# Local transformer: the output product right behind the scores, the residual sum behind the first shift

## The chip, the cores and the metric

The kernel runs on one core of one Trainium2 chip. The metric is the device time of one execution in microseconds. Five engines work from instruction queues of their own: TensorE (PE, matrix products), VectorE (DVE), ScalarE (ACT), GpSimd (POOL) and SyncE (SP, which here issues all the DMAs). They meet only through semaphores.

## The reference, cut to what matters

The whole program is two layers of a model on 2 x 1024 tokens of 128 features: time mixing with a scan, then a local transformer of depth 6, then full attention, then a mixture of experts. The change touches the local transformer alone:

```python
for i in range(DEPTH):                                   # 6
    x = attn_layer(shift_tokens(x), Wqkv[i], q_scale[i], k_scale[i], Wo[i]) + x
    x = ffn_layer(shift_tokens(x), ln_g[i], ln_b[i], W1[i], b1[i], W2[i], b2[i]) + x

def attn_layer(x, Wqkv, qs, ksc, Wo):                    # 16 heads of 64
    q, k, v = heads(x @ Wqkv)
    q, k = l2norm(q) * qs, l2norm(k) * ksc
    q, k = rotary(q), rotary(k)
    out = local_attention(q, k, v)                       # windows of 32, each sees itself and the one before
    return out @ Wo
```

The moved product is `out @ Wo`, and the moved sum is the `+ x` behind it.

## The kernel before, in words

All of it is unrolled. The local transformer works on groups of 128 tokens: 16 groups (SLOTS) in each of 6 layers, 96 in all, with even groups of one batch and odd ones of the other. A chunk is a pair of groups, and the feed-forward part works on chunks. The order of the work is written out by hand: each engine has a loop over steps i (STEPS), and in a step it does its part for several groups that stand at different depths of the pipeline. What keeps engines apart is semaphores that count finished operations.

A step i of TensorE, in this order (the line is that of the product itself): turn 0 and turn 1, transposes of rotated queries of group i (`turn_qk`, L624); qk 0 and qk 1, projections of group i+2 (`project_qk`, 512 columns each, in three products L607 to L609); turn 2 and 3 for the keys; qk 2 and 3; in odd steps the variance for the feed-forward norm (L717); the attention's output of group i-2 transposed (`turn_att`, L692); the scores of group i (L643 mask, L653, 128 small products); the probabilities of group i-1 transposed (`turn_prob`, L664); one half of v for group i+1 (`project_v`, L607 to L609); in even steps the second feed-forward product (`down`, L735); the other half of v; the value products of group i-1 (`weigh_v`, L682, 128 small ones); in even steps the centre product (L712), in odd ones three pairs of `up` products (L726, L727); last, `project_out` of group i-2 (L704, eight products of the program, 16 passes).

Four banks of PSUM, TURN, are shared in turn by turn, qk, att, prob, v, down, up and out. The dictionary `uses` numbers their uses in TensorE's order, and `wait_free` makes use n wait until the reader of use n-4 is done. Scores and values use three banks of their own.

ScalarE empties turn (L1024), qk (L977), att (L1035), prob (L1030) and v (L1009); it squares queries and keys (L985), takes exponents (L1041), and computes the norms from the sums of squares (L999, L1001, L1003, at the end of a step, for group i+2). In odd steps it also applies the gate's Gelu (L1068), which has a table of its own: one load ahead of it, and one behind it (L1070) for the table of Ln and Exp. In some even steps it splits weights of the next layer (L970).

VectorE in a step: `normalise` of group i+1 (L1296, L1303), first half of `shift_scores` of group i (row maximum L1316, difference L1318), `sum_probs` of group i-1 (L1327; in odd steps it stands ahead of the shift), norm of the feed-forward (L1353, odd) or `finish` (L1367, even, which reads the down product), the second half of `shift_scores`, the sum of squares of group i+2 (L1289), `norm_att` of the first half of group i-1 (L1337), the three `hidden` products (L1359, odd), `add_residual` of group i-2 (L1343), `norm_att` of the second half.

GpSimd rotates group i+1 (L514 products, L519 sums) behind `normalise`, and does the low parts of split weights (L479) and tokens. SyncE issues loads of weights and tokens, the copies of v into windows (`load_v`), and f_x, the feed-forward's input (`load_f_x`, which waits until the residual sums of both groups of a chunk are done).

Of the kernel before, what the change touches and what calls it, by code (L numbers as in the profile page):

```python
# [74 lines left out]
def time_mixing_and_local(nc, A, sb, sem, bank, ident, mean_w, eps, x_main, h_in, h_mid, mod, gate_a):  # L75

    ALL = LAYERS * SLOTS
# [5 lines left out]
    with ExitStack() as ctx:  # L83
# [142 lines left out]
        def live(g):  # L226
            return 0 <= g < ALL

        def even(i, back):
            c = (i - back) // 2  # L230
            return c if (i - back) % 2 == 0 and 0 <= c < CHUNKS else None
# [34 lines left out]
        uses = {}  # L266
        for i in STEPS:
            for a in range(2):
                for j in (2 * a, 2 * a + 1):
                    if live(i):  # L270
                        uses["turn", i, j] = len(uses)
                for j in (2 * a, 2 * a + 1):
                    if live(i + 2):
                        uses["qk", i + 2, j] = len(uses)
            if live(i - 2):
                uses["att", i - 2, 0] = len(uses)
                uses["att", i - 2, 1] = len(uses)
            if i - 2 == ALL - 1:
                uses["out", i - 2, 0] = len(uses)
            if live(i - 1):  # L280
                uses["prob", i - 1, 0] = len(uses)
                uses["prob", i - 1, 1] = len(uses)
            if live(i + 1):
                uses["v", i + 1, 0] = len(uses)
            if even(i, 6) is not None:
                uses["down", even(i, 6), 0] = len(uses)
            if live(i + 1):
                uses["v", i + 1, 1] = len(uses)
            if even(i, 5) is not None:
                for j in range(FB):  # L290
                    uses["up", even(i, 5), j] = len(uses)
            if live(i - 2) and i - 2 < ALL - 1:
                uses["out", i - 2, 0] = len(uses)
        order = list(uses)

        def turn_bank(*use):
            return TURN[uses[use] % len(TURN)]
# [34 lines left out]
        def wait_layer(eng, layer):  # L332
            eng.wait_ge(s_layer[layer % 2], 64 * (layer // 2 + 1))

        with nc.Block(no_gpsimd_drain=True) as blk:
# [264 lines left out]
            def _(pe):  # L600
# [95 lines left out]
                def project_out(g):  # L696
                    layer = g // SLOTS
                    if g % SLOTS == 0:
                        wait_layer(pe, layer)
                    wait_free(pe, "out", g, 0)  # L700
                    pe.wait_ge(S.att_out, 2 * (g + 1))
                    o = bank[:, turn_bank("out", g, 0), 0:BLK]
                    for hp in range(PAIRS):
                        mm = pe.matmul(o, w_o[:, layer % 2, hp, :], att_t[:, g % 2, hp, :], start=hp == 0,  # L704
                                       stop=hp == PAIRS - 1)
                    mm.then_inc(S.out, 1)
# [193 lines left out]
                for i in STEPS:  # L900
                    if i == -1:
                        group_mean(3)
                        project_output(2)
                        second_mean(2)
                        group_var(3)
                        second_var(2)
                    if i == 0:
                        project_output(3)
                        second_mean(3)
                    for a in range(2):  # L910
                        for j in (2 * a, 2 * a + 1):
                            if live(i):
                                turn_qk(i, j)
                        for j in (2 * a, 2 * a + 1):
                            if live(i + 2):
                                project_qk(i + 2, j)
                        if i == 0 and a == 0:
                            second_var(3)
                    if even(i, 5) is not None:
                        variance(even(i, 5))  # L920
                    if live(i - 2):
                        turn_att(i - 2, 0)
                        turn_att(i - 2, 1)
                    if i == ALL + 1:
                        project_out(ALL - 1)
                        last_mean(0)
                    if live(i):
                        scores(i)
                    if live(i - 1):
                        turn_prob(i - 1, 0)  # L930
                        turn_prob(i - 1, 1)
                    if live(i + 1):
                        project_v(i + 1, 0)
                    if i == ALL + 2:
                        center(CHUNKS - 1)
                    if even(i, 6) is not None:
                        down(even(i, 6))
                    if i == ALL + 2:
                        last_var(1)
                    if i == ALL + 3:  # L940
                        last_mean(2)
                    if i == ALL + 4:
                        last_mean(3)
                        last_var(3)
                    if i == ALL + 5:
                        last_mean(4)
                        last_var(4)
                    if live(i + 1):
                        project_v(i + 1, 1)
                    if live(i - 1):  # L950
                        weigh_v(i - 1)
                    if even(i, 4) is not None and i != ALL + 2:
                        center(even(i, 4))
                    if even(i, 5) is not None:
                        for j in range(FB):
                            up(even(i, 5), j)
                    if i == ALL + 1:
                        last_var(0)
                        last_mean(1)
                    if i == ALL + 3:  # L960
                        last_var(2)
                    if live(i - 2) and i - 2 < ALL - 1:
                        project_out(i - 2)

            @blk.scalar
            def _(act):
# [317 lines left out]
            def _(dve):  # L1284
# [255 lines left out]
                for i in STEPS:  # L1540
                    if i == -1:
                        add_logs(3)
                    if live(i + 1):
                        normalise(i + 1)
                    if i == -1:
                        second_scale(2)
                        group_norm(3)
                    if i == 0:
                        second_scale(3)
                        modulation(1)  # L1550
                    if live(i - 1) and even(i - 1, 5) is None:
                        sum_probs(i - 1)
                    if live(i):
                        shift_scores(i, 0)
                    if live(i - 1) and even(i - 1, 5) is not None:
                        sum_probs(i - 1)
                    if i == ALL + 1:
                        last_sum(0)
                        last_sum(1)
                    if even(i, 5) is not None:  # L1560
                        norm(even(i, 5))
                    if i == ALL + 1:
                        add_residual(ALL - 1)
                        last_sum(2)
                    if i == ALL + 2:
                        last_scale(0)
                    if i == ALL + 3:
                        last_scale(1)
                    if even(i, 6) is not None:
                        finish(even(i, 6))  # L1570
                    if i == ALL + 2:
                        last_sum(3)
                    if i == ALL + 4:
                        last_sum(4)
                        last_scale(3)
                    if i == ALL + 5:
                        last_scale(4)
                    if live(i):
                        shift_scores(i, 1)
                    if live(i + 2):  # L1580
                        sum_squares(i + 2)
                    if i == -1:
                        add_output(3)
                    if live(i - 1):
                        norm_att(i - 1, 0)
                    if even(i, 5) is not None:
                        for j in range(FB):
                            hidden(even(i, 5), j)
                    if i == ALL + 3:
                        last_scale(2)  # L1590
                    if live(i - 2) and i - 2 < ALL - 1:
                        add_residual(i - 2)
                    if live(i - 1):
                        norm_att(i - 1, 1)
                dve.wait_ge(S.ff_out, CHUNKS)
# [1078 lines left out]
```

## Time and profile before

| | us |
|---|---|
| median of 3 runs | 2623.19 |
| lowest and highest | 2614.48, 2628.58 |
| the profiled execution's own time | 2625.65 |
| its span | 2623.9 |
| busy: TensorE | 2453.0 (93%) |
| busy: VectorE | 2159.1 (82%) |
| busy: ScalarE | 2037.2 (78%) |
| busy: GpSimd | 1518.5 (58%) |

The span is from the first to the last instruction of one profiled execution. The mean granted clock of TensorE over it is 0.984, where 1 is 2.4 GHz. The local transformer takes most of the span, from about 120 to 1650 us; full attention and the experts follow.

### The profile page before, as it was taken

What the parts mean: (1) busy time and instruction counts of PE and PEld (TensorE: products, weight loads), DVE (VectorE), ACT (ScalarE), POOL (GpSimd) and SP (SyncE); (2) the same over time, 40 slices, a digit from 0 to 9 for tenths busy, and PEclk for the clock granted to TensorE, in tenths of its full rate; (3) what the DMA queues carried; (4) which work ended last, traced back from release to release, by engine and by line L of the source; (5) the groups of instructions that cost most, each with busy time, mean ns of one, the idle gap of its engine ahead of it and who ended that gap; (6) DMA issues with size and microseconds to landing.
All of it is one profiled execution on the core that took longest, in us unless ns stands there. A gap on an engine that the chain in (4) does not pass through costs nothing. (4 is left out here: it accounts for less than half of the span.)

```text
span 2623.9 us, 118567 instructions
## 1 busy us (share of the span) xinstructions
PE 2453.0 (93%) x52349; PEld 1966.4 (75%) x52349; DVE 2159.1 (82%) x2455; ACT 2037.2 (78%) x4077; POOL 1518.5 (58%) x1029
## 2 busy tenths in 40 slices
PE   6799999999999999999999999689999999997999
PEld 2488888888888888888888887467676776775787
DVE  5888888888888888888888887388888888885888
ACT  4688888889889888888888887566666666764676
POOL 3788887888788878888788785122222232322111
PEclk9899999999999999999999999899999999999999
DMA  3243433443334334333433333122222222221221
GB/s 96 56 94 92 106 77 92 92 106 83 93 93 113 80 89 102 96 83 93 97 94 79 85 85 71 36 54 52 60 61 58 50 61 60 57 53 34 82 73 41
DMA packets 275793, 202.01 MB, mean 77 GB/s; under 512 B 117568, under 2 KB 215880, under 8 KB 274248
## 3 DMA queue, kind: packets, MB, share of 16 engines
q1 hardware_dynamic: 275280, 194.42, 30.9%
q8 instruction: 414, 6.78, 1.1%
q14 instruction: 99, 0.81, 0.1%
HBM read 36.96 MB, written 1.11 MB: 15 GB/s over the span
## 5 line engine op out<-in xcount | busy, mean ns | idle before, releaser
L514 POOL TENSOR_TENSOR lt_t_sin<-lt_qk,lt_tab 128x512 f32<-128x512 f32 x384 | 682.8, 1799 | 243.9 <-DVE lt_qk L1296 241.8
L519 POOL TENSOR_TENSOR lt_qr<-lt_qr,lt_t_sin 128x1024 f32<-128x1024 f32 x192 | 457.8, 2385 | 28.2 <-POOL lt_t_sin L514 0.5
L2078 DVE TENSOR_REDUCE fa_neg_max<-bank 128x1 f32<-128x1024 f32 x256 | 301.6, 1220 | 94.7 <-PE bank L1875 93.3
L1901 PE MATMUL bank<-fa_prob_t,fa_v 32*64 32x128 f32 x16384 | 295.9, 277 | 18.9 <-issue 14.0
L2000 ACT ACTIVATE fa_prob<-bank,fa_neg_max 128x1024 f32<-128x1024 f32 x128 | 142.7, 1115 | 217.5 <-DVE fa_neg_max L2078 165.2
L1901 PEld LDWEIGHTS bank<-fa_prob_t,fa_v 32*64 32x64 f32 x16384 | 245.8, 131 | 81.3 <-issue 60.5
L2088 DVE STREAM_TRANSPOSE fa_prob_t<-fa_prob 128x1024 f32<-128x1024 f32 x256 | 302.1, 1219 | 0.0
L607 PE MATMUL bank<-lt_w_high,lt_x_high 128*128 128x512 f32 x576 | 262.8, 456 | 0.8 <-ACT lt_v_tok L1009 0.4
L1296 DVE TENSOR_TENSOR lt_qk<-lt_qk,lt_rn 128x2048 f32<-128x2048 f32 x96 | 236.3, 2461 | 5.9 <-ACT lt_rn L1003 2.2
L1289 DVE TENSOR_REDUCE lt_ssq<-lt_qr 128x32 f32<-128x2048 f32 x96 | 218.9, 2281 | 23.0 <-ACT lt_qr L985 23.0
L1303 DVE TENSOR_TENSOR lt_qr<-lt_qk,lt_tab 128x2048 f32<-128x2048 f32 x96 | 232.7, 2424 | 3.3
L977 ACT COPY lt_qk<-bank 128x512 f32<-128x512 f32 x384 | 220.4, 593 | 18.2 <-POOL lt_t_sin L514 2.8
L608 PE MATMUL bank<-lt_w_low,lt_x_high 128*128 128x512 f32 x576 | 228.4, 396 | 0.0
L609 PE MATMUL bank<-lt_w_high,lt_x_low 128*128 128x512 f32 x576 | 227.8, 396 | 0.0
L1316 DVE TENSOR_REDUCE lt_row_max<-bank 128x8 f32<-128x512 f32 x192 | 131.7, 686 | 113.4 <-PE bank L653 113.4
L624 PE MATMUL bank<-ident,lt_qr 128*128 128x128 f32 x1536 | 201.1, 274 | 14.7 <-POOL lt_qr L519 12.6
L985 ACT ACTIVATE lt_qr<-lt_qk 128x1024 f32<-128x1024 f32 x192 | 203.4, 1060 | 0.0
L624 PEld LDWEIGHTS bank<-ident,lt_qr 128*128 128x128 f32 x1536 | 177.5, 141 | 31.4 <-POOL lt_qr L519 15.7
L704 PEld LDWEIGHTS bank<-lt_prob_t,lt_w_o 128*128 128x128 f32 x1536 | 186.7, 192 | 8.1 <-issue 1.5
L704 PE MATMUL bank<-lt_prob_t,lt_w_o 128*128 128x128 f32 x1536 | 187.6, 275 | 1.0 <-ACT lt_prob_t L1035 0.8
L1807 POOL TENSOR_TENSOR fa_att_t<-fa_att,fa_inv_all 128x512 f32<-128x512 f32 x32 | 40.6, 1270 | 245.4 <-ACT fa_att L2024 245.4
L682 PEld LDWEIGHTS bank<-lt_v,lt_prob_t 64*32 64x32 f32 x12288 | 130.1, 105 | 66.7 <-issue 65.1
(260 smaller groups left out, 5912.5 us busy)
## 6 DMA issues: line engine op xcount, KB each, us to landing
lt_v<-lt_v_tok SPq DMA_DIRECT2D x576, 128.0 KB
fa_v<-fa_v_tok SPq DMA_DIRECT2D x256, 128.0 KB, 2.7
lt_v<-lt_v_tok SPq DMA_DIRECT2D x192, 64.0 KB
lt_k_t<-lt_k_t SPq DMA_DIRECT2D x84, 128.0 KB, 2.7
lt_v<-lt_v SPq DMA_DIRECT2D x168, 64.0 KB, 2.1
lt_w_raw<-in_lt_wqkv_dram SPq DMA_DIRECT2D x36, 256.0 KB
ex_cw_all<-cw_kept SPq DMA_DIRECT2D x8, 1024.0 KB, 4.5
lt_x_s<-h_in SPq DMA_DIRECT2D x96, 64.0 KB, 2.7
```

The lines of the kernel that those rows point to most:

```text
L514: pool.tensor_tensor(dst[:, :, i, :], src[:, :, 1 - i, :], tab[:, g // 2 % 2, 1, at:at + 32].unsqueeze(1).to_broadcast([P, HEADS, 32]), AL ...
L519: pool.tensor_tensor(qr[:, g % 2, half], qr[:, g % 2, half], t_sin[:, :], ALU.add).then_inc(S.rotated, 1)
L607: pe.matmul(o, xh, w_high[:, k % WS, :], start=True, stop=False)
L608: pe.matmul(o, xh, w_low[:, k % WS, :], start=False, stop=False)
L609: return pe.matmul(o, xl, w_high[:, k % WS, :], start=False, stop=True)
L624: mm = pe.transpose(bank[:, turn_bank("turn", g, j), n * P:(n + 1) * P], qr[:, g % 2, (4 * j + n) * P:(4 * j + n + 1) * P], ident[:, :])
L704: mm = pe.matmul(o, w_o[:, layer % 2, hp, :], att_t[:, g % 2, hp, :], start=hp == 0, stop=hp == PAIRS - 1)
L1296: dve.tensor_tensor(heads, heads, r.unsqueeze(2).to_broadcast([P, 2 * HEADS, HD]), ALU.mult)\
L1303: dve.tensor_tensor(qr[:, g % 2, :].rearrange("p (a h d) -> p a h d", a=2, h=HEADS), qk[:, g % 2, :].rearrange("p (a h d) -> p a h d", a=2 ...
L1901: mm = pe.matmul(bank[d, 4 + a, 0:P].rearrange("p (u r) -> p u r", u=UPQ), v[rows, half % 2, kb, d], prob_t[rows, q % 2, par, :, 32 * kb:3 ...
L2078: dve.tensor_reduce(neg_max[:, u % 2, par:par + 1], bank[:, 2 * par:2 * par + 2, :].rearrange("p a n -> p (a n)"), AX.X, ALU.max, negate=T ...
L2088: dve.transpose(prob_t[:, q % 2, par, u % UPQ, :], prob[:, u % 2, par, :]).then_inc(S.turned, 1)
```

## The change

The call of `project_out(i - 2)` moves on TensorE from the end of the step to the place right behind `scores(i)`, ahead of `turn_prob(i - 1, 0)`. The call of `add_residual(i - 2)` moves on VectorE from between `hidden` and the second `norm_att` to right behind `shift_scores(i, 0)`. The list `uses` moves its entry of "out" along, to stand behind "att" and ahead of "prob", so that the numbering of bank uses stays that of TensorE's order; with it every use behind "att" in the step gets another bank and another predecessor. The last group (ALL - 1) had its own, earlier place already and keeps it. No instruction is added or taken away.

```diff
@@ uses
             if live(i - 2):
                 uses["att", i - 2, 0] = len(uses)
                 uses["att", i - 2, 1] = len(uses)
-            if i - 2 == ALL - 1:
+            if live(i - 2):
                 uses["out", i - 2, 0] = len(uses)
@@
                 for j in range(FB):
                     uses["up", even(i, 5), j] = len(uses)
-            if live(i - 2) and i - 2 < ALL - 1:
-                uses["out", i - 2, 0] = len(uses)
@@ TensorE
                     if live(i):
                         scores(i)
+                    if live(i - 2) and i - 2 < ALL - 1:
+                        project_out(i - 2)
                     if live(i - 1):
                         turn_prob(i - 1, 0)
@@
-                    if live(i - 2) and i - 2 < ALL - 1:
-                        project_out(i - 2)
@@ VectorE
                     if live(i):
                         shift_scores(i, 0)
+                    if live(i - 2) and i - 2 < ALL - 1:
+                        add_residual(i - 2)
                     if live(i - 1) and even(i - 1, 5) is not None:
                         sum_probs(i - 1)
@@
-                    if live(i - 2) and i - 2 < ALL - 1:
-                        add_residual(i - 2)
                     if live(i - 1):
                         norm_att(i - 1, 1)
```

## Rows read from the trace of the kernel before

**Rows 1.** Busy time by stretch: us of stretch, then each engine; PEclk, DMA share, GB/s.
```profile
900.00:1100.00 200.00, 192.56 (x4177) 164.26 (x4175) 167.47 (x178) 176.62 (x328) 163.08 (x92) 1.00 0.41 96
```

**Rows 2.** Waits of TensorE, 140 to 1660 us: total us, times, longest.
```profile
PE bank L682 <- issue: 24.7, 25, 1.9
PE bank L664 <- ACT lt_prob L1041: 13.7, 23, 1.8
PE bank L653 <- issue: 4.7, 6, 2.5
```

**Rows 3.** Timeline, TensorE, odd into even step: start, us, what; idle before in brackets.
```profile
1023.05 0.59 PE L727 MATMUL bank<-lt_f_norm,lt_w 128*85 128x256 f32 x2
1023.48 1.95 PE L704 MATMUL bank<-lt_prob_t,lt_w_o 128*128 128x128 f32 x16
1025.27 1.04 PE L624 MATMUL bank<-ident,lt_qr 128*128 128x128 f32 x8
...
1027.54 1.03 PE L624 MATMUL bank<-ident,lt_qr 128*128 128x128 f32 x8
1028.33 0.48 PE L607 MATMUL bank<-lt_w_high,lt_x_high 128*128 128x512 f32 x1
```

**Rows 4.** Timeline, ScalarE, the same boundary.
```profile
1023.69 0.47 ACT L1068 ACTIVATE lt_f_gate<-bank,lt_lvec 85x256 f32<-85x256 f32 x1 [0.39 <-PE bank L727]
1024.18 1.28 ACT L1070 ACT_TABLE_LOAD   x1
...
1026.31 0.57 ACT L1024 COPY lt_q_t<-bank 128x512 f32<-128x512 f32 x1
...
1027.26 0.60 ACT L977 COPY lt_qk<-bank 128x512 f32<-128x512 f32 x1
```

**Rows 5.** Timeline, TensorE, the even step and into the next.
```profile
1031.10 1.48 PE L653 MATMUL bank<-lt_k_t,lt_q_t 64*32 64x64 f32 x128
1033.19 1.09 PE L664 MATMUL bank<-ident,lt_prob 128*128 128x128 f32 x8 [0.61 <-ACT lt_prob L1041]
...
1036.91 1.48 PE L682 MATMUL bank<-lt_v,lt_prob_t 64*32 64x64 f32 x128
...
1042.92 1.03 PE L624 MATMUL bank<-ident,lt_qr 128*128 128x128 f32 x8
1043.71 0.48 PE L607 MATMUL bank<-lt_w_high,lt_x_high 128*128 128x512 f32 x1
```

**Rows 6.** Timeline, VectorE, the end of the even step.
```profile
1036.33 0.49 DVE L1367 SCALAR_TENSOR_TENSOR h_in<-bank,lt_lvec,h_mid 128x256 f32<-128x256 f32 x1 [0.77 <-PE bank L735]
...
1038.05 2.27 DVE L1289 TENSOR_REDUCE lt_ssq<-lt_qr 128x32 f32<-128x2048 f32 x1
...
1040.85 0.29 DVE L1343 TENSOR_TENSOR h_mid<-h_in,bank 128x128 f32<-128x128 f32 x1
```

**Rows 7.** Timeline, ScalarE, even into odd step.
```profile
1040.36 0.32 ACT L999 ACTIVATE lt_rn<-lt_ssq,lt_least 128x32 f32<-128x32 f32 x1 [1.40 <-DVE lt_ssq L1289]
...
1041.47 0.58 ACT L1024 COPY lt_q_t<-bank 128x512 f32<-128x512 f32 x1
...
1042.50 0.59 ACT L977 COPY lt_qk<-bank 128x512 f32<-128x512 f32 x1
```

**Rows 8.** Timeline, TensorE, value products of two odd steps.
```profile
1053.80 0.27 PE L682 MATMUL bank<-lt_v,lt_prob_t 64*32 64x64 f32 x2 [1.59 <-issue]
...
1273.40 1.09 PE L664 MATMUL bank<-ident,lt_prob 128*128 128x128 f32 x8
...
1275.83 1.17 PE L682 MATMUL bank<-lt_v,lt_prob_t 64*32 64x64 f32 x96
1278.90 0.46 PE L682 MATMUL bank<-lt_v,lt_prob_t 64*32 64x64 f32 x32 [1.90 <-issue]
```

**Rows 9.** Timeline, GpSimd, end of the second rotation.
```profile
1039.80 2.37 POOL L519 TENSOR_TENSOR lt_qr<-lt_qr,lt_t_sin 128x1024 f32<-128x1024 f32 x1
```

**Rows 10.** Busy time in the stretch behind the hole of 1.90 us.
```profile
1280.40:1283.70 3.30, 3.30 (x10) 2.27 (x9) 0.97 (x2) 0.95 (x2) 2.46 (x2) 0.50 0.26 60
```

## The prediction

> **What bounds the kernel now.** I read the busy time of the engines in a stretch of the local stage first. TensorE is busy 192.56 of 200 us there, ScalarE 177, VectorE 167, GpSimd 163 [rows 1]. So TensorE sets the pace and an edit can give back only its few idle microseconds. The waits of TensorE over the whole stage (140 to 1660 us) say what those are: 24.7 us inside the value products L682 and 4.7 us inside the scores L653, both with nobody to wait for ("issue"), and 13.7 us ahead of the probability transposes L664, on the exponent [rows 2]. The moved product L704 appears in no large wait: where it stands it waits for nothing.
>
> The timeline then shows a strict pattern of two steps. An odd step ends with the three "up" products, an even one with the centre product; both then run L704, and the next step starts. L704 holds TensorE for 1.79 us, from 1023.48 to the next start at 1025.27, and as long in the other step [rows 3]. Meanwhile other engines do what the start of the next step needs. The question is therefore less what the product fills at its new place than what it covered at the old one.
>
> **What is needed at a step's start.** The four turning banks go round: use n waits until use n-4 is emptied. A step begins turn 0, turn 1, qk 0, qk 1, turn 2, turn 3, qk 2, qk 3. So turn 2 waits for ScalarE's copy of turn 0, and qk 2 for its copy of qk 0, and TensorE reaches turn 2 only 2.27 us after its step began (1025.27 to 1027.54). The change alters no link among these eight.
>
> *Odd to even.* The last up product starts at 1023.05; the gate on it at 1023.69, after ScalarE idled 0.39 us for it, so this chain is released by TensorE. Behind it on ScalarE without a hole: gate, 1.28 us of table load at 1024.18, three small norm operations, two copies of turned queries, and the copy of qk 0 from 1027.26 to 1027.86 [rows 4]. TensorE starts qk 2 at 1028.33 [rows 3]. Spare: 0.47 us. With L704 gone from between, TensorE arrives 1.79 us sooner after the up product, while the chain is as long as before. It needs about 0.05 us from a copy's end to the start (the exponent's release shows such a lag). Stall: 1.79 - 0.47 + 0.05 = 1.37 us. Of this 1.2 us show already at turn 2 (the copy of turn 0 ends at 1026.88, turn 2 starts at 1027.54), the rest at qk 2.
>
> *Even to odd.* Here VectorE carries it. The "down" product is followed by the sum L1367 at 1036.33, for which VectorE idled 0.77 us; then the second shift and the sum of squares from 1038.05 to 1040.32 [rows 6]. ScalarE idled 1.40 us for that sum, then runs the norms, the square L1045, two copies (the first from 1041.47 to 1042.05), and the copy of qk 0 from 1042.50 to 1043.09 [rows 7]. TensorE starts qk 2 at 1043.71 [rows 5]: 0.62 us to spare. The down product stands behind the new place of L704 too, so again the anchor comes 1.79 us nearer: 1.79 - 0.62 + 0.05 = 1.22 us.
>
> I read these two spares step by step. In 39 of 44 even steps the first is 0.5 to 0.6 us; in the other five, at the end of a layer, a weight copy on ScalarE leaves 0.05. In 41 of 44 odd steps the second is 0.5 to 0.6 us, in three 0.2. Each odd step from 5 on has the gate behind it and each even one from 6 on the down product, so 45 boundaries of each kind count: 45 x (1.37 + 1.22) = 116.6 us, and the tighter ones add 5 x 0.4 + 3 x 0.4 = 3.2. **Cost: 120 us.** Both anchors are on TensorE and lie behind the preceding stall, so one stall does not pay for the next. Lower bound: if only half came through, 60; upper: no spare at all, 1.79 at each, 161.
>
> **What the new place gives.** In an even step the scores end near 1032.6, and the transposes L664 start at 1033.19 after 0.61 us idle [rows 5]. The exponent that they wait for stands behind split copies and copies of the turned attention. With 1.79 us of product between, the wait is covered: 18 even steps lose about 0.7 us now, the others 0 to 0.4. In the row they are 13.7 us [rows 2]: **-14 us** (bounds 10 and 20).
>
> The product itself waits at its new place for the attention's copies out of the turning banks (ScalarE, which works on them while the scores run) and for bank use n-4, now qk 2: long emptied. Cost nothing; without the cover some tenths a step. Its first weight load waits no more than before.
>
> The "issue" idle is a second gain. It comes in the middle of 128 identical tiny products, as 96 of them, 1.90 us of nothing, then 32 [rows 8]. It falls nearly all in odd steps, where from the transposes L664 to L682 there are 2.43 us (1273.40 to 1275.83) [rows 8]; in even steps the down product makes that 3.72 us (1033.19 to 1036.91) [rows 5], with the wait ahead of it, and the idle is nearly gone. I take it that instructions arrive no faster, and two bursts of 256 instructions stand too close. The move puts 1.79 us (and 32 instructions) between them. Of 29.4 us [rows 2], which may be somewhat more with idle under the table's threshold, I take **-22 us** (bounds 0 and -35).
>
> The Trainium skill, "Runtime: NRT & Kernel Launch", section "Instruction fetch mechanics", speaks against this term: it says that fetch is hidden, since the sequencer issues more slowly than its buffer fills. By it the idle would have another cause, nothing says that it would shrink, and the sum would be 22 us higher. The trace has idle without a releaser in the burst, so I weigh the page as a rival only.
>
> **The other moved parts.** add_residual is 0.29 us of VectorE, at 1040.85 of the even step [rows 6], where it used to hold up the second norm_att. Now it stands behind the first shift and may wait there: shift done some 1.5 us after the scores, product 1.8 us and its signal after them, so up to 0.5 us of waiting. Behind it are queued sum_probs or the layer's norm, finish and the second shift. In even steps finish waits 0.77 us for the down product anyway, and that comes later too: hidden. In odd steps the second shift feeds only the next scores: hidden. Without that cover it is 0.5 us in 96 steps. The freed end of the step does not start normalise sooner, since that also waits for the norms, which come later by the chains above.
>
> GpSimd's rotation follows normalise. Its last sum ends at 1039.80 + 2.37 = 1042.17 and turn 2 of the odd step starts at 1042.92 [rows 5, 9]: 0.75 us spare. The rotation moves 1.8 us later, TensorE 1.37 - 0.68 later in this step: short by 0.4 us, under the 1.0 us that turn 2 then waits for ScalarE anyway. Cost nothing, unless the bank chain is shorter than I think; then 0.4 us in 20 steps.
>
> Bank uses shift: down waits for the residual sum in its own step (done some 2.4 us after the scores; the transposes and a projection still lie ahead of down), and qk 1 of even steps for the last hidden product, just in time, and if late, under the wait that follows at turn 2. SyncE's f_x load waits for the sum that is now earlier, and its value loads, issued behind v's copy, are 1.8 us later with a step to go before use. Nothing for either.
>
> **Sum.** On the profiled execution's own 2625.65 us (span 2623.9): + 120 - 14 - 22 = 2709.6 us. That execution lies 2.5 us above the median of the runs, so 2707; since some stalls will give instruction supply time ahead of the scores, I take 2704 us, 3.1% slower.
>
> **Rivals.**
> - *The boundary absorbs the loss* (faster, 0.07). The single mechanism: ScalarE's and VectorE's chains run earlier than rows 4, 6 and 7 tell, because they are not released by the up and down products. Then only the gains count: 2623 - 14 - 22 = 2587. It decides where the delay of the qk 0 copy is under 0.5 us. Against it: the idle rows directly ahead of the gate, of L1367 and of L999 show all three waiting. A half-way version, with one of the two boundaries free, gives 2707 - 55 = 2652 (0.12).
> - *Supply idle stays* (0.17): 2704 + 22 = 2726. For it: only an inference from spacing backs the gain.
> - *The clock falls* (0.06). In one step the 1.90 us hole in L682 is followed by a stretch of granted clock 0.50, 3.3 us long, and 1.00 again behind it [rows 8, 10]. At half clock such a stretch loses some 1.7 us. If one pair in two brought it: 2704 + 24 x 1.7 = 2745. Against it: the hole of 1.59 us at 1052 lies in 200 us of clock 1.00 [rows 1, 8], with the 0.61 us holes of that stretch; the new ones are under 1.4 us. The Trainium skill, "TensorE: Matmul & The Clock Gate", section "A second HAM failure mode: psum-queue depth-cycling", describes just this, short idle at each turn of the banks that makes the clock swing; the trace has so far not borne it out.
> - *Nothing moves* (0.04): the product is 1.8 us wherever it stands, and all is absorbed: 2620.
>
> **Numbers.** Forecast 0.54 at 2704. The range from 2650 takes in one free boundary, and up to 2735 lost supply gains. Under about 0.5% this kernel's measurement can't tell a change. Faster 0.07, same 0.04, slower 0.89.
>
> **What would show it.** Right: waits of TensorE L624 on ScalarE's copy lt_q_t L1024, some 1 us, in nearly every step, 90 or more in all, with a smaller one at L607; the wait of L664 on the exponent gone; the issue idle in L682 well under 24.7 us; TensorE busy down to 182 to 186 of 200 us in the stretch of rows 1; pairs of steps 1.5 to 2 us longer. Wrong: L624 without such waits, or waiting on GpSimd's lt_qr instead; clock 0.5 in the stage's windows; a wait of L704 itself on lt_prob_t.

## The result and the profile after

The changed kernel takes 2719.78 us (median of 4 runs, 2713.29 to 2722.47) against 2625.89 us (2614.48 to 2633.98) for the kernel before, measured with it. The ratio is 1.0357, 95% interval 1.0313 to 1.0402: 3.6% slower. The profiled execution has a span of 2719.3 us, 95.4 us more than before. Its lines from the bank numbering on stand two lower: L622 is the L624 of before (turn), L702 the L704 (output product), L680 the L682 (value products), L651 the L653 (scores).

The instructions are the same in number and kind. TensorE is busy 91% instead of 93%, in the stretch of [rows 1] 187.45 us instead of 192.56, at the same granted clock:

```profile
PE 2484.1 (91%) x52349; PEld 1960.2 (72%) x52349; DVE 2145.8 (79%) x2455; ACT 2015.7 (74%) x4077; POOL 1517.3 (56%) x1029
```
```profile
900.00:1100.00 200.00, 187.45 (x4004) 156.01 (x4003) 156.59 (x172) 162.64 (x305) 153.01 (x89) 1.00 0.35 82
```

TensorE's waits in the local stage, here 140 to 1760 us, answer to [rows 2]:

```profile
PE bank L622 <- ACT lt_q_t L1022: 79.0, 89, 1.6
PE bank L651 <- issue: 12.5, 15, 2.3
PE bank L680 <- issue: 10.8, 20, 2.1
PE bank L622 <- POOL lt_qr L517: 4.0, 3, 1.5
...
PE bank L702 <- issue: 3.7, 7, 0.7
```

A wait that is not in [rows 2] now comes 89 times: turn 2 waits for ScalarE's copy of turn 0. The wait of 13.7 us on the exponent is gone. The idle without a releaser (called supply idle below) is no longer mainly inside the value products; the scores now have more of it.

The odd-to-even boundary answers to [rows 3, 4]. First TensorE, then ScalarE. The up product is now followed at once by turn 0, and turn 2, due 2.27 us later, comes 3.54 us later (1082.45 to 1085.99), 0.14 us after ScalarE's copy of turn 0 (from 1085.28, 0.57 us, the first of the two in the row) has ended. The third up product still releases the gate, and the chain behind it has kept its length:

```profile
1082.02 0.59 PE L725 MATMUL bank<-lt_f_norm,lt_w 128*85 128x256 f32 x2
1082.45 1.32 PE L622 MATMUL bank<-ident,lt_qr 128*128 128x128 f32 x8
...
1085.99 1.07 PE L622 MATMUL bank<-ident,lt_qr 128*128 128x128 f32 x8 [0.65 <-ACT lt_q_t L1022]
1086.87 0.50 PE L605 MATMUL bank<-lt_w_high,lt_x_high 128*128 128x512 f32 x1
```
```profile
1082.65 0.47 ACT L1066 ACTIVATE lt_f_gate<-bank,lt_lvec 85x256 f32<-85x256 f32 x1 [0.27 <-PE bank L725]
1083.14 1.28 ACT L1068 ACT_TABLE_LOAD   x1
...
1085.28 1.05 ACT L1022 COPY lt_q_t<-bank 128x512 f32<-128x512 f32 x2
...
1086.22 0.60 ACT L975 COPY lt_qk<-bank 128x512 f32<-128x512 f32 x1
```

The copy of qk 0 ends at 1086.82, and the product that needs its bank starts at 1086.87: the spare of 0.47 us is used up. Note the bracket: 0.65 us, while the start is 1.27 us late. The group of turn 0 and 1 has itself become longer (1.32 instead of 1.04 us), as turn 1 waits a little for VectorE's first hidden product, which reads the bank that turn 1 needs; such pieces of a late start stand in no bracket of turn 2. The distance between two starts is the safer reading.

The even-to-odd boundary answers to [rows 5 to 7], TensorE, VectorE, ScalarE:

```profile
1098.56 1.04 PE L622 MATMUL bank<-ident,lt_qr 128*128 128x128 f32 x8
...
1101.90 1.06 PE L622 MATMUL bank<-ident,lt_qr 128*128 128x128 f32 x8 [0.90 <-ACT lt_q_t L1022]
```
```profile
1093.15 0.29 DVE L1341 TENSOR_TENSOR h_mid<-h_in,bank 128x128 f32<-128x128 f32 x1 [0.47 <-PE bank L702]
...
1096.03 0.48 DVE L1365 SCALAR_TENSOR_TENSOR h_in<-bank,lt_lvec,h_mid 128x256 f32<-128x256 f32 x1 [1.17 <-PE bank L733]
...
1097.76 2.27 DVE L1287 TENSOR_REDUCE lt_ssq<-lt_qr 128x32 f32<-128x2048 f32 x1
```
```profile
1100.07 0.32 ACT L997 ACTIVATE lt_rn<-lt_ssq,lt_least 128x32 f32<-128x32 f32 x1 [1.41 <-DVE lt_ssq L1287]
...
1101.18 1.06 ACT L1022 COPY lt_q_t<-bank 128x512 f32<-128x512 f32 x2
```

The copy of turn 0 again is the first of the last row's two (0.58 us), and turn 2 again starts 0.14 us after its end. The residual sum waits 0.47 us at its new place, and that costs nothing here: VectorE then waits 1.17 us for the down product in any case.

For the experiments I call the time from the start of turn 0 to the start of turn 2 the head of a step. It is 2.27 us where nothing waits (0.87 us in step 94, which has no projection between). Summed over 45 even steps (6 to 94) and 44 odd ones (7 to 93):

| kernel | heads even | heads odd | supply idle (L682, L653) |
|---|---|---|---|
| before | 101.1 | 100.0 | 24.7, 4.7 |
| changed | 159.5 | 144.7 | 10.8, 12.5 |

### The profile page after: what moved, and what is told of

It is laid out like the page before. It is cut to its first block and busy times, and to the rows that moved or that the text cites. A ratio compares the mean times of both kernels' runs of the same rounds, so it can differ in the third digit from the quotient of the medians.

```text
span 2719.3 us, 118567 instructions
## 1 busy us (share of the span) xinstructions
PE 2484.1 (91%) x52349; PEld 1960.2 (72%) x52349; DVE 2145.8 (79%) x2455; ACT 2015.7 (74%) x4077; POOL 1517.3 (56%) x1029
## 5 line engine op out<-in xcount | busy, mean ns | idle before, releaser
L1899 PEld LDWEIGHTS bank<-fa_prob_t,fa_v 32*64 32x64 f32 x16384 | 246.8, 131 | 78.7 <-issue 58.4
L622 PE MATMUL bank<-ident,lt_qr 128*128 128x128 f32 x1536 | 210.9, 277 | 96.7 <-ACT lt_q_t L1022 81.1
L622 PEld LDWEIGHTS bank<-ident,lt_qr 128*128 128x128 f32 x1536 | 172.7, 142 | 156.2 <-issue 101.6
L1294 DVE TENSOR_TENSOR lt_qk<-lt_qk,lt_rn 128x2048 f32<-128x2048 f32 x96 | 222.1, 2313 | 48.6 <-ACT lt_rn L1001 48.4
L1028 ACT COPY lt_prob_t<-bank 128x512 f32<-128x512 f32 x192 | 103.3, 590 | 176.5 <-PE bank L662 176.5
L975 ACT COPY lt_qk<-bank 128x512 f32<-128x512 f32 x384 | 214.1, 629 | 6.3 <-POOL lt_t_sin L512 2.8
L1314 DVE TENSOR_REDUCE lt_row_max<-bank 128x8 f32<-128x512 f32 x192 | 131.6, 686 | 101.1 <-PE bank L651 100.9
L702 PE MATMUL bank<-lt_prob_t,lt_w_o 128*128 128x128 f32 x1536 | 199.4, 283 | 5.3 <-issue 3.7
L702 PEld LDWEIGHTS bank<-lt_prob_t,lt_w_o 128*128 128x128 f32 x1536 | 180.6, 193 | 15.7 <-issue 7.3
```

The lines of the kernel that those rows point to most:

```text
L622: mm = pe.transpose(bank[:, turn_bank("turn", g, j), n * P:(n + 1) * P], qr[:, g % 2, (4 * j + n) * P:(4 * j + n + 1) * P], ident[:, :])
L1294: dve.tensor_tensor(heads, heads, r.unsqueeze(2).to_broadcast([P, 2 * HEADS, HD]), ALU.mult)\
L1899: mm = pe.matmul(bank[d, 4 + a, 0:P].rearrange("p (u r) -> p u r", u=UPQ), v[rows, half % 2, kb, d], prob_t[rows, q % 2, par, :, 32 * kb:3 ...
```

## The experiments

Ratios are to the kernel before, timed on the same chip beside each experiment, with the 95% interval in brackets; a time in us is the median. The medians of before were 2622 to 2633, so across experiments the ratio is the safer measure. Diffs are shortened, with ... for what is left out. The waits shown are those of 140 to 1680 us.

**e1, the new places in even steps only.** Both calls and the entry of "out" get a condition:

```diff
-                    if live(i - 2) and i - 2 < ALL - 1:
+                    if live(i - 2) and i - 2 < ALL - 1 and i % 2 == 0:
                         project_out(i - 2)      # behind scores(i); with != at the step's end
```

> The kernel before, with the product and the residual sum at their new places in even steps only; odd steps end with the product as before. Theory (cover at the step boundary): only the even-to-odd boundary loses its cover. In the changed kernel the heads of odd steps (start of turn 0 to start of turn 2) and the gap to qk 2 grew by 48.6 us in sum; against that the wait ahead of the probability transposes in even steps goes, about 16 us. So +33 us (20 to 45), heads of odd steps 3.3 us, of even steps 2.3 us. Rival (the cost lies at the new place: residual sum behind the first shift, other banks): even steps carry half of the 95 us and the heads are not what grew, +45 to +50 us with waits elsewhere. Rival (one boundary alone matters, the gate's): this kernel is faster than before by about 16 us.

Measured: 2671.01 us, ratio 1.0164 (1.0130 to 1.0198), +43 us.

**e2, the same in odd steps only.**

> The kernel before, with the product and the residual sum at their new places in odd steps only. Theory: the odd-to-even boundary loses its cover, heads of even steps go from 2.3 to 3.5 us (62 us in sum with qk 2), no wait is filled in odd steps: +62 us (50 to 70), heads of odd steps unchanged. Together with the even-only kernel the two differences should add up to the 94 us of the whole change. Rival (supply idle shrinks with the distance of the two bursts, as I predicted): up to 20 us less, +42. Rival (cost at the new place): +45 to +50 like its sister.

Measured: 2682.75 us, ratio 1.0209 (1.0175 to 1.0243), +55 us. TensorE's waits of e1, then of e2:

```profile
PE bank L624 <- ACT lt_q_t L1026: 39.0, 46, 1.4
PE bank L682 <- issue: 32.9, 34, 1.8
PE bank L653 <- issue: 9.3, 10, 2.5
```
```profile
PE bank L624 <- ACT lt_q_t L1026: 40.1, 44, 1.6
PE bank L664 <- ACT lt_prob L1043: 14.9, 33, 0.7
PE bank L682 <- issue: 12.3, 21, 1.2
PE bank L653 <- issue: 9.4, 10, 2.3
```

The heads separate cleanly. In e1 the odd ones sum to 144.6 us and the even ones to 101.0; in e2 the even ones to 159.4 and the odd ones to 100.0: each boundary pays for its own lost cover, as much as in the whole change, and the other pays nothing. 43 + 55 = 98 us, against 94 for both together; both are inside what I expected. In e1 the wait on the exponent is gone and the heads cost 48 us with qk 2; the rest of its +43 is supply idle, 42.2 us in these rows against 29.4. In e2 it fell, to 21.7.

**e3 and e4, no function table.** Relu for Gelu, and the reload left out, in the changed kernel and in the one before.

```diff
-                        act.activation(f_gate[0:m, j, :], ..., ACT.Gelu,
+                        act.activation(f_gate[0:m, j, :], ..., ACT.Relu,
...
-                    act.preload_act_table_set("natural_log_exp_and_others")
```

> The changed kernel with Relu in place of Gelu in the feed-forward gate, so that ScalarE loads no function table (two loads of 1.28 us in each odd step go). It computes another activation. Theory: the chain up product, gate, table load, norms, copies is 1.28 us shorter than the 1.3 us stall needs: heads of even steps fall from 3.5 back to about 2.3 us, heads of odd steps stay at 3.3 us; 2720 - 55 = 2665 us. Rival (turn 2 waits for something else, such as VectorE's or GpSimd's work): under 10 us gained.

> The kernel before with Relu in place of Gelu, the control for the changed kernel with Relu. It computes another activation. Theory: before, the table loads lay under the product at the step's end, so their removal gains nearly nothing: within 8 us of before. Rival: ScalarE bounds the kernel as a whole and the loads cost their 48 x 1.28 to 2.57 us everywhere: 60 us or more faster.

Measured: e3 2657.70 us, ratio 1.0123 (1.0086 to 1.0161), 62 us under the changed kernel. e4 2617.97 us, ratio 0.9967 (0.9951 to 0.9983), 10 us under before, just outside the 8 us that I expected. Heads of even steps in e3 sum to 112.6 us instead of 159.5, of odd ones to 145.8. Its waits have the 46 of the odd steps left:

```profile
PE bank L622 <- ACT lt_q_t L1022: 39.9, 46, 1.4
PE bank L651 <- issue: 11.0, 16, 1.2
PE bank L680 <- issue: 8.3, 17, 1.1
```

So the same edit gives back 10 us where the output product lay over the table loads, and about 62 us where it doesn't. The 10 us of e4 are not at the heads, which stay at 101.1 us, and their place stays open. Of the 62 us, 47 are in the even heads. What is left of the stall there, 11.5 us, is mostly (7.4) the wait of turn 1 for the first hidden product, which the bracket of turn 2 hid.

**e5, a shorter sum of squares** in the changed kernel.

```diff
-    qr[:, g % 2, :].rearrange("p (h d) -> p h d", d=HD), AX.X, ALU.add)
+    qr[:, g % 2, :].rearrange("p (h d) -> p h d", d=HD)[:, :, 0:HD // 2], AX.X, ALU.add)
```

> The changed kernel with VectorE's sum of squares over the first half of each head alone (L1287, 2.28 us to some 1.2). It leaves out half of the squares of each norm. Theory: on the even-to-odd boundary the chain is down product, finish, second shift, sum of squares, norms, copies; it gets 1.1 us shorter and heads of odd steps fall from 3.3 to about 2.3 us, heads of even steps (the gate's chain, on ScalarE) stay at 3.5: 2720 - 45 = 2675 us. Rival (both stalls hang on ScalarE's gate and table): no change of odd heads, under 10 us gained. Rival (VectorE's total is the bound): both heads fall, 80 us or more.

Measured: 2684.79 us, ratio 1.0182 (1.0131 to 1.0232), against 1.0357: some 46 us less. Heads of odd steps sum to 106.4 us instead of 144.7, of even steps to 159.1 as in the changed kernel. That is as expected. It is VectorE's sum that the odd heads hang on, though the wait names ScalarE's copy.

**e8, light copies of v,** in the kernel before: each copy takes one of eight head pairs. One run.

```diff
-  sp.dma_start(v[lo:lo + 2 * WIN, g % 2, w, :, :], src[WIN * (w - 1):WIN * (w + 1)])
+  sp.dma_start(v[lo:lo + 2 * WIN, g % 2, w, 0:1, :], src[WIN * (w - 1):WIN * (w + 1), 0:1])
```

> The kernel before with the copies of v into windows cut to one eighth of their bytes (same number of copies and same waits; the value products then read partly old v). It tests whether the supply idle comes from DMA traffic that delays the instruction blocks. Rival (traffic): the idle without a releaser inside L682 and L653 falls from 29 us to under 12. Otherwise it stays at 25 to 33 us, and the distance in instructions alone matters.

Measured: 2641.18 us in its one execution, where before took 2625 to 2645 us beside it: no difference that can be told. Its waits:

```profile
PE bank L682 <- issue: 28.1, 31, 2.0
...
PE bank L653 <- issue: 5.8, 9, 2.8
```

33.9 us against 29.4, somewhat above the 25 to 33 that I expected and far from the rival's 12: the idle in the bursts does not come from the traffic of these copies.

**e7, value products behind the up products** in odd steps, from the kernel before.

```diff
- if live(i - 1): weigh_v(i - 1)
+ if live(i - 1) and i % 2 == 0: weigh_v(i - 1)      # TensorE, the old place
  center, up
+ if live(i - 1) and i % 2 != 0: weigh_v(i - 1)      # the same for norm_att(i - 1, 0) and hidden on VectorE
```

> The kernel before, with the value products behind the up products in odd steps (and the first norm_att behind the hidden products), so that 2.7 us more lie between the bursts of scores and of value products. It tests my failed term, the supply idle. Spacing theory: idle inside L682 (24.7 us before) falls under 8 us and does not come back elsewhere, 15 to 20 us faster. Rival (idle belongs to the block boundaries of the instruction stream, which fall on a burst sooner or later): it moves to the scores and other places, total idle without a releaser stays at 27 to 33 us, time within 8 us of before.

Measured: 2632.20 us, ratio 0.9992 (0.9977 to 1.0007): no difference. Its waits:

```profile
PE bank L726 <- ACT lt_f_norm L1060: 22.3, 47, 1.5
PE bank L664 <- ACT lt_prob L1043: 10.2, 19, 1.8
PE bank L682 <- issue: 7.8, 10, 1.3
PE bank L653 <- issue: 6.5, 10, 1.3
```

I expected 15 to 20 us. By the time alone the rival would have won. By the rows the supply idle did fall, from 29.4 to 14.3 us (in the value products to 7.8, under the 8 that I expected), and a new wait took the place: the up products now come before their normalised input is ready.

**e9, that wait taken out,** by order alone:

```diff
+ if even(i, 5) is not None: norm(even(i, 5))            # VectorE: now ahead of shift_scores(i, 0)
+ if even(i, 5) is not None: shift_norm(even(i, 5))      # ScalarE: now ahead of empty_prob(i - 1, 0)
```

> The value products behind the up products in odd steps as in the run of that name, and the wait it made (L726 on the normalised input, 22.3 us in sum) taken out by order: the feed-forward norm ahead of the first shift on VectorE, its shift ahead of the probabilities' copies on ScalarE. Theory: supply idle stays at the lower 14 to 16 us (it was 29.4 before) and nothing new waits: 15 to 20 us faster than before. Rival (supply idle comes back elsewhere): within 5 us of before.

Measured: 2599.04 us, ratio 0.9891 (0.9864 to 0.9918): 1.1% faster than before, 29 us (21 to 36), more than the 15 to 20 expected. Its rows tell of 16 us less supply idle (13.2), 3 less of waiting on the exponent, and the 2.8 us that before idles without a releaser ahead of up products are gone; the rest stays open.

```profile
PE bank L664 <- ACT lt_prob L1043: 10.3, 19, 1.8
PE bank L682 <- issue: 8.7, 17, 1.8
PE bank L653 <- issue: 4.5, 8, 0.7
```

**e6 and e10, another filler for the exponent's wait:** in even steps the first v projection and its copy stand ahead of the probability transposes and their copies; e6 from the kernel before, e10 from e9.

```diff
+ if live(i + 1) and i % 2 == 0: project_v(i + 1, 0)     # empty_v and uses likewise
  turn_prob(i - 1, 0), turn_prob(i - 1, 1)
+ if live(i + 1) and i % 2 != 0: project_v(i + 1, 0)
```

> The kernel before, with the first v projection (and its copy on ScalarE) ahead of the probability transposes in even steps, where those wait for the exponent. The step's end keeps the output product. Theory: a filler that does not come out of the boundary's cover takes the 0.1 to 0.7 us waits and costs nothing: before - 15 us (8 to 20). Rival: the probabilities' copies come 0.6 us later on ScalarE and hold the value products: no gain, or up to 10 us slower.

> The same with the first v projection ahead of the probability transposes in even steps as well. Alone that gave 4.5 us, as its trace had 12 us more supply idle. If the two ends of the idle are separate: another 8 to 15 us below the kernel without it, 25 to 30 us under before. Rival (supply idle eats it again): 0 to 5 us.

Measured: e6 2628.02 us, ratio 0.9978 (0.9959 to 0.9997), some 5 us instead of the 15 (8 to 20) expected; e10 2597.96 us, ratio 0.9873 (0.9845 to 0.9900), not told apart from e9, where I expected another 8 to 15. Both are misses. Of the wait of L664 on the exponent one of 1.8 us is left in each. The gain was eaten by supply idle, as the rival for e10 had it: in e10 that is 18.8 us against 13.2 in e9, and in e6 (L684 and L655 are its value products and scores) it rose by 12 us:

```profile
PE bank L684 <- issue: 34.0, 32, 2.7
...
PE bank L655 <- issue: 7.5, 9, 2.8
```

**e11, the output product's move once more, where value products end the odd step.** e9 with the edit of e2.

> The same order (value products last in odd steps, norm early), and with it the output product and the residual sum at their new places in odd steps. In the order of before this move cost 55 us. Theory (only the work behind the up product counts as cover): 1.5 us of value products now cover the gate's chain, so the spare of 0.47 us before shrinks by 0.3 us and no stall comes: within 8 us of the kernel of this order without the move. Rival (the product's new place itself, its bank or the residual sum behind the first shift costs): 30 to 55 us slower than that kernel again.

Measured: 2638.43 us, ratio 1.0035 (1.0017 to 1.0053), 39 us above e9: outside what I expected, and inside the rival's 30 to 55, by which the new place itself costs. The time alone does not tell a cost of the place from a chain that I had read wrongly; the heads and e12 do. Heads of even steps sum to 126.4 us (101.0 in e9). Where the chain comes from is in the timeline, TensorE and then ScalarE:

```profile
1022.00 1.04 PE L664 MATMUL bank<-ident,lt_prob 128*128 128x128 f32 x8
...
1031.34 1.06 PE L624 MATMUL bank<-ident,lt_qr 128*128 128x128 f32 x8 [0.48 <-ACT lt_q_t L1028]
```
```profile
1022.98 1.08 ACT L1034 COPY lt_prob_t<-bank 128x512 f32<-128x512 f32 x2 [1.79 <-PE bank L664]
1023.94 0.60 ACT L1013 COPY lt_v_tok<-bank 128x512 f32<-128x512 f32 x1
1024.41 1.08 ACT L989 ACTIVATE lt_qr<-lt_qk 128x1024 f32<-128x1024 f32 x1
1025.37 0.60 ACT L1013 COPY lt_v_tok<-bank 128x512 f32<-128x512 f32 x1
1025.99 1.28 ACT L1072 ACT_TABLE_LOAD   x1
1027.28 1.20 ACT L1072 ACTIVATE lt_f_gate<-bank,lt_lvec 128x256 f32<-128x256 f32 x3
1028.49 1.28 ACT L1074 ACT_TABLE_LOAD   x1
```

ScalarE works without a hole from 1022.98 to the copies of turn 0 and qk 0. In this order the gate no longer waits for the up products (three of them in 1.20 us, no idle), so the start of the chain is the last wait before it: 1.79 us, for the probability transposes. The product was moved from behind that point to ahead of it.

**e12, the same with the squares of the keys in that wait.**

```diff
  shift_norm(even(i, 5))
+ if live(i + 2) and i % 2 != 0: square_qk(i + 2, 1)      # was behind empty_v(i + 1, 0)
  empty_prob(i - 1, 0), empty_prob(i - 1, 1)
```

> The kernel with value products last, norm early and the output product moved in odd steps (2638 us), with one more reordering: in odd steps ScalarE squares the keys (1.04 us) ahead of the probabilities' copies, in the 1.79 us in which it waits for the probability transposes. Theory now: in that kernel the chain to the copies of turn 0 and qk 0 starts at the probability transposes, not at the last up product; the output product was moved from behind that start to ahead of it, and the even heads stall for 0.6 us (sum 126 against 101). A chain 1.04 us shorter leaves no stall: heads of even steps back to 2.3 us, 25 to 35 us faster than 2638, within 15 us of the kernel without the product's move (2599). Rival (the product's new place costs by itself, through its bank or the residual sum on VectorE): no more than 10 us gained.

Measured: 2610.04 us, ratio 0.9954 (0.9938 to 0.9969). That is 28 us under e11 by the medians, but e11 and e12 were not timed together; by the ratios it is 0.8%, 21 us (15 to 28), under the 25 to 35 expected and well over the rival's 10. Heads of even steps sum to 104.6 us; L624 has no wait on ScalarE among the large ones any more:

```profile
PE bank L664 <- ACT lt_prob L1045: 10.7, 19, 1.8
PE bank L682 <- issue: 10.5, 19, 1.1
PE bank L653 <- issue: 9.5, 10, 1.4
```

So most of the product's cost at its new place in odd steps was the chain that it no longer covered, but not all: by the ratios e12 is still 17 us above e9 (11 by the medians). Of that the even heads hold 3.6 us, and supply idle is 20.0 us instead of 13.2; the rest is not traced, and some cost of the new place itself is not excluded.

## Why the prediction was right, step by step

*The direction and the mechanism.* Predicted: TensorE gets back to the banks 1.79 us sooner after the up and the down product, and ScalarE's copies are not ready. The rows of the changed kernel show it, e1 and e2 show that the two boundaries pay separately, e3 and e5 that shortening either chain alone gives back that boundary alone.

*The cost of the boundaries, +120 us.* Measured with qk 2 counted in: even steps 62.2 us (58.4 in the head, 3.8 at qk 2), for which I had 45 x 1.37 and 2 for the layer ends, 64; odd steps 48.6 us, for which I had 55 and 1. Together 111. The odd term was 7 us too big, for three reasons. The most common stall is 1.15 us and not 1.22, some 3 us in all; 44 such boundaries count and not 45; and where a supply hole falls into the value products of an even step, it comes behind the down product and itself gives the chain time. In eleven odd steps of the changed kernel the head is 0.1 to 0.7 us shorter for that, 4 us in all.

*The exponent's wait, -14 us.* Gone, as predicted: start to start it was some 16 us.

*The supply idle, -22 us.* This is the step that failed. All waits of TensorE without a releaser sum to 33.1 us before and 29.2 after, 4 us less and not 22. The value products lost 13.9 us of it [rows 2] and the scores gained 7.8, the output product 3.7 at its new place. I had assumed that idle belongs to the pair of bursts; e6 and e1, in which it rose by 12 and 13 us, show that it comes back elsewhere. The rival "supply idle stays", 2726 us, was nearer to the 2720 measured than my 2704. The forecast came as near as it did partly by luck: two terms were too dear by 11 us together (the boundaries and the exponent's wait), which hid half of the 18 that this one lacked. The last 3 us, taken off for stalls that give the supply time, have no run behind them either.

*The page of the Trainium skill.* "Runtime: NRT & Kernel Launch", section "Instruction fetch mechanics", says that fetch is hidden by the issue rate. The runs don't bear that out: holes of up to 2.5 us stand inside bursts of identical products, and always where a block of 256 instructions ends (last section). Its consequence for the sum, no gain from the spacing, came nearer than mine all the same, though not for the page's reason.

*The moved sum, bank uses, GpSimd, SyncE: nothing.* Right in sum. The residual sum waits 0.47 us under cover. L622 waits for GpSimd's rotation 4.0 us in sum, three times; before it was 3.1 us, also three times. In the working for that term the 0.68 us names no row, so its shortfall of 0.4 us cannot be followed; the runs show 0.9 us in sum. Turn 1 of even steps waits 7.2 us in sum for the first hidden product; that comes under the wait of turn 2, and I had named qk 1 and not turn 1 for it.

*The clock.* 1.00 in the stretch of rows 1, mean over the span 0.985 against 0.984: that rival fell.

*The signs.* The waits of L624 came (89), the wait on the exponent went, the supply idle in the value products fell to 10.8 us, and a pair of steps is 2.1 us longer (34.2 instead of 32.0), just over the 1.5 to 2 forecast. TensorE's 187.45 us of 200 lie above the 182 to 186 that I had named.

*The sum.* 111 - 16 - 4 = 91 us; the spans differ by 95.4. The other 4 us stay open.

## What to carry to other kernels

A piece of work on the engine that sets the pace may cover a chain on other engines even if no row ever shows a wait there. Before moving it, find what starts that chain (the last row with an idle bracket ahead of it), and count whether the work stood behind that start and now stands ahead of it: here 1.79 us of cover against a spare of 0.47 and 0.62 us, 89 times. After each reordering look for that start anew, as e11 shows. And fill a wait, if at all, with work from the same side of that start: e6 and e10 did so and left the heads alone, but their gain was 5 us at most. Closing a small wait is not yet a gain while another idle can take its place.

## What the runs showed of the hardware

TensorE's instructions arrive in blocks. Of the queues that carry instructions one fits its count; in the changed kernel:

```profile
q8 instruction: 414, 6.78, 1.0%
```

TensorE has 106014 instructions in the trace, 104698 products and weight loads and 1316 others; over 414 packets these are 256 each. I counted TensorE's instructions up to each idle of over 0.5 us without a releaser in the local stage: 24 of 24 before and 22 of 22 after lie at the same count modulo 256 (to within one instruction), that is at a block's end. Of the 24 before, 21 stood in the value products or the scores, where a burst uses a block in 1.5 us, and three in the up products. So where a hole falls is set by which instruction happens to end a block, and any reordering moves it: one order differs from another by 10 us or more in this term (L682 and L653 together 14.3 us in e7, 42.2 in e1).

The packets of that queue say more. In the stage of the kernel before no two of them start less than 3.3 us apart, and 26 starts of TensorE's products come over 0.6 us late at a block's end: each of these is 2.2 to 3.0 us after the start of the latest packet, and 1.0 to 1.5 us after its end. So such a wait ends a short time after a block has landed, as a wait for that block would. A block that lasts 1.5 us is thus used up faster than blocks come, which fits two bursts too close to each other; so does the low supply idle in each kernel with value products last in odd steps (13.2 to 20.0 us in e7, e9 to e12). But the changed kernel has 23.3 us and e2 21.7 without that order, and so this order is not what the amount hangs on alone. What starts a packet stays open; e8 excludes only the copies of v.
